# Own terms of a graph attention layer added behind the merge instead of inside it

## The chip, the cores and the metric

One core of one Trainium2 chip runs the whole program. The metric is the device time of one execution in microseconds (us), as the median of several executions. TensorE, VectorE, ScalarE, GpSimd and SyncE are called PE, DVE, ACT, POOL and SP, as in the profile.

## The reference, cut to what matters

Four graph layers follow each other on 3125 nodes with 256 features; 53125 edges (src, dst, sorted by dst) contain a self loop for each node. The change touches only the fourth, an attention layer with 8 heads of 32 features, which adds a self loop to each node once more:

```python
loop = jnp.arange(n); src = jnp.concatenate([src, loop]); dst = jnp.concatenate([dst, loop])
h = (x @ W).reshape(n, HEADS, OUT_DIM)
e = jax.nn.leaky_relu(a_src[src] + a_dst[dst], 0.2)
m = jax.ops.segment_max(e, dst, num_segments=n)
e = jnp.exp(e - m[dst])
denom = jax.ops.segment_sum(e, dst, num_segments=n)
alpha = e / (denom[dst] + 1e-16)
out = jax.ops.segment_sum(h[src] * alpha[:, :, None], dst, num_segments=n)
# + bias, an inner layernorm with gamma and beta, then layernorm(x + out)
```

The kernel takes this second self loop apart: for every node it adds an "own term", its own row h times exp(own score - maximum of its segment), to the sum over the listed edges. A row has 264 floats: 8 heads of 32 features and a 1 behind each, so that the denominator is summed beside the numerator.

## The kernel before

Nodes lie in 25 tiles of 128, edges in 416 tiles of 128; four edge tiles are a quad (104 quads). The last stage, the **merge**, sums weighted source rows into node tiles. For each quad the rows h[src] are brought into one of 16 row places (4 tiles, 528 KB). Places 1, 3, 5, ... 15 and 8 are staged: their rows were gathered early, kept in DRAM, and SP loads them back with one DMA each (`load_rows`, L2155). The seven other places are direct: POOL gathers their rows with four indirect DMAs for each quad (`gather_group`, L2105). A place is used again 16 quads later; `place_free` makes SP and POOL wait until `s_mm`, which PE counts up by one at every step (it starts at 8), shows that the old rows have been read: quad q waits for count 8 + 4(q - 16) + 3 + 25.

DVE weighs the rows of a quad in place (`scale_rows`, L2461) and builds onehot matrices for a group of four steps (`node_hots`, L2467), in two halves of one buffer, so group q waits until PE's count is 4q + 4, which is reached when group q - 2 is through. PE then does one fp32 matmul for each step (L2506, two instructions in the trace), 440 steps or 110 groups in all; a node tile is summed in one of four PSUM banks. ACT waits for the end of each node tile, copies its bank out (L2523) and prepares the bank of the node tile four further on. DVE's order is hots of group q, rows of quad q + 1, hots of group q + 1, and so on; nothing else stands in its queue until the last group.

The own term enters like this. Ahead of the merge each edge's segment maximum is written to DRAM. At the start of the merge POOL gathers first quads 6, 10, 12 and 14, then the maximum of each node tile (`gather_last`, L2428, 25 indirect DMAs), then makes the exponents (`weigh_own`, L2433 and L2435), and only then gathers the direct quads from 16 on. SP loads all own rows (3.3 MB, L2445) between the first and the second round of staged places. ACT takes the exponential (L2532) and weighs own rows by head (`weigh`, L2518, eight instructions for one node tile): those of tiles 8 to 24 straight into the bank, ahead of its sums, those of tiles 0 to 7 in place, beside copies of their sums, which DVE adds behind the merge (L2551).

Behind the merge `attended`, `inner_stats`, `inner_norm` and `store` run over groups of four node tiles, each stage one group behind the one before. DVE's order is attended(0); inner_stats(0), attended(1); inner_norm(0), inner_stats(1), attended(2); and so on. inner_norm(0) waits for a square root that ACT makes (L763), and ACT's root stands in its queue behind everything that `merge_act` issues.

## Time and profile before

| | |
|---|---|
| median of 3 executions | 3052.11 us (3040.15 to 3060.54) |
| the profiled execution, its own time | 3039.42 us |
| its span, first to last instruction | 3037.6 us |
| mean granted TensorE clock | 0.906 of full speed |
| merge, first weighing of rows to the last copy of a bank | 2625.5 to 2966.8 us |
| behind the merge | 2966.8 to 3037.6 us |
| busy share of the span | PE 81%, DVE 46%, POOL 31%, ACT 23% |

All places in time are microseconds from the start of the span. In a timeline a row gives start, duration, engine, line, operation, tiles, how many instructions are merged, and in brackets how long the engine was idle before it and who ended that. "remote" is an end of a wait for which the profile finds no instruction; "issue" is time without a wait that it shows. A DMA issued by POOL counts as busy only while its descriptors are made.

### The profile page before, as it was taken

Reading aid. Unit: us, or ns where it says so; the run is one execution under the profiler, and the core shown is the slowest. Engines: PE = TensorE matmul, PEld = TensorE weight load, DVE = VectorE, ACT = ScalarE, POOL = GpSimd, SP = SyncE. Lnnn points to the kernel's source line nnn. Section 1 sums busy time; section 2 is a strip of 40 time slices with the busy share of each in tenths; the row PEclk is TensorE's granted clock in tenths of the full one; section 3 lists DMA queues with packets and bytes.
Section 4 is the critical chain, followed back from the end, with each engine's and each line's share of the span. In section 5 each row is a group of like instructions: output and inputs, shape, how many; then the busy total and the mean of one; then the engine's idle time right before and its main releaser. Section 6 shows DMA issues by size and latency. Waiting matters only on the chain. (4 is left out here: it accounts for less than half of the span.)

```text
span 3037.6 us, 32378 instructions
## 1 busy us (share of the span) xinstructions
PE 2471.0 (81%) x9483; PEld 1629.1 (54%) x9484; DVE 1394.4 (46%) x3940; ACT 708.7 (23%) x1552; POOL 932.0 (31%) x927
## 2 busy tenths in 40 slices
PE   4777988996884999999999999999947787547680
PEld 2444977434763555565556555677723344435560
DVE  7998755455673001030101001455636555636568
ACT  3777644112442000010001000354400000103112
POOL 0000256665664300000000000012267665566640
PEclk8898998997996999999999999999978989769885
DMA  6656677343332544444444444333287888536541
GB/s 234 246 238 253 198 233 217 126 144 120 111 105 71 167 153 129 156 132 148 135 150 131 149 124 140 103 98 103 77 213 252 266 269 261 188 111 198 179 134 42
DMA packets 209534, 493.89 MB, mean 163 GB/s; under 512 B 46457, under 2 KB 128430, under 8 KB 209134
## 3 DMA queue, kind: packets, MB, share of 16 engines
q1 hardware_dynamic: 134353, 297.50, 30.6%
q10 hardware_dynamic: 39005, 137.07, 13.3%
q0 software_dynamic: 36032, 57.60, 7.1%
q8 instruction: 67, 1.10, 0.1%
q14 instruction: 77, 0.63, 0.1%
HBM read 374.71 MB, written 117.32 MB: 162 GB/s over the span
## 5 line engine op out<-in xcount | busy, mean ns | idle before, releaser
L792 POOL DMA_INDIRECT table_dense_weights<-pair_weight,dst x416 | 408.5, 982 | 607.8 <-DVE weights_c L845 350.6
L1522 PE MATMUL banks<-own_term,features_and_rows 128*128 128x391 f32 (+1 forms) x1656 | 552.3, 491 | 0.0
L2105 POOL DMA_INDIRECT features_and_rows<-table_heads,src x376 | 399.6, 1063 | 223.4 <-issue 105.8
L1522 PEld LDWEIGHTS banks<-own_term,features_and_rows 128*128 128x128 f32 x1656 | 312.2, 189 | 226.8
L1548 DVE TENSOR_SCALAR features_and_rows<-banks,hop_bias 128x391 f32<-128x391 f32 (+1 forms) x24 | 15.0, 624 | 780.2 <-PE banks L1522 780.2
L947 PE MATMUL banks<-split_rows,count_columns 128*128 128x512 f32 x1200 | 320.5, 415 | 17.5 <-issue 9.3
L2506 PE MATMUL banks<-features_and_rows,edge_to_window 128*128 x880 | 232.3, 426 | 107.9 <-DVE edge_to_window L2467 60.0
L1522 PE MATMUL banks<-features_and_rows 128*128 128x391 f32 (+1 forms) x840 | 282.4, 491 | 0.0
L947 PEld LDWEIGHTS banks<-split_rows,count_columns 128*128 128x128 f32 x1200 | 228.6, 194 | 70.9 <-issue 15.6
L2506 PEld LDWEIGHTS banks<-features_and_rows,edge_to_window 128*128 128x128 f32 x880 | 180.2, 209 | 159.9 <-issue 126.2
L558 PE MATMUL banks<-features_and_rows,pair_and_bias_rows 128*128 128x400 f16 x806 | 185.3, 395 | 85.4 <-DVE features_and_rows L540 41.3
L929 ACT CAST count_columns<-hidden 128x640 fp32r<-128x640 f16 x310 | 212.7, 723 | 144.5 <-PE banks L947 41.8
L1522 PEld LDWEIGHTS banks<-features_and_rows 128*128 128x128 f32 x840 | 158.4, 189 | 114.6
L2197 PE MATMUL banks<-features_and_rows,pair_weight 128*104 128x512 bf16 (+1 forms) x672 | 170.9, 395 | 58.8 <-issue 36.7
L1973 POOL DMA_INDIRECT ble_values_at_first_edge<-dst,row_of_first_edge x50 | 48.1, 961 | 515.1 <-DVE ln_rstd L1952 449.6
L1597 POOL DMA_INDIRECT features_and_rows<-table_hop,node_of_tail_row x6 | 5.7, 952 | 630.9 <-DMA table_hop<-tmp 609.6
L558 PEld LDWEIGHTS banks<-features_and_rows,pair_and_bias_rows 128*128 128x128 f16 x806 | 113.8, 152 | 157.2 <-issue 142.7
L540 DVE TENSOR_SCALAR features_and_rows<-counter_fp,features_and_rows 128x400 f16<-128x400 f16 x806 | 196.9, 320 | 0.0
L1539 ACT ACTIVATE features_and_rows<-banks,hop_bias 128x391 f32<-128x391 f32 (+1 forms) x24 | 14.1, 587 | 724.6 <-PE banks L1522 724.6
L2197 PEld LDWEIGHTS banks<-features_and_rows,pair_weight 128*104 128x104 bf16 x672 | 90.3, 138 | 161.0 <-issue 103.7
L1067 PE MATMUL banks<-split_rows,count_columns 128*128 128x258 f32 (+1 forms) x1200 | 160.7, 293 | 13.9 <-issue 9.3
L1067 PEld LDWEIGHTS banks<-split_rows,count_columns 128*128 128x128 f32 x1200 | 154.5, 199 | 18.0 <-issue 16.4
(425 smaller groups left out, 2985.8 us busy)
## 6 DMA issues: line engine op xcount, KB each, us to landing
hidden<-table_counts SPq DMA_DIRECT2D x305, 160.0 KB
table_dense_weights<-weights_c ACTq DMA_DIRECT2D x26, 1600.0 KB, 5.7
own_term<-table_dense_weights SPq DMA_DIRECT2D x52, 782.0 KB
features_and_rows<-table_rows_by_edge SPq DMA_DIRECT2D x58, 528.0 KB
pair_and_bias_rows<-table_edge_rows ACTq DMA_DIRECT2D x52, 512.0 KB
weights_c<-table_edge_rows ACTq DMA_DIRECT2D x52, 512.0 KB
own_term<-table_dense_weights SPq DMA_DIRECT2D x34, 780.5 KB
table_rows_by_edge<-features_and_rows SPq DMA_DIRECT2D x48, 528.0 KB
```

The lines of the kernel that those rows point to most:

```text
L540: made = e.tensor_scalar(hot_ring[:, s % HOTS, q, :], counter[:, 0:WIDE], steps_key[:, q, s:s + 1], None, ALU.is_equal)
L558: m = e.matmul(banks[:, bass.ds(bank_at, WIDE)], low_ring[:, s // LOWS_AT_ONCE % LOW_BLOCKS, :, 2 * (s % LOWS_AT_ONCE) + q], hot_ring[:, s ...
L792: e.indirect_dma_start(out=self.table, out_offset=bass.IndirectOffsetOnAxis(ap=self.place[:, t:t + 1], axis=0), in_=self.values[:, t:t + 1 ...
L929: e.copy(in_group(count_columns, g), in_group(slot_of(q), g)).then_inc(s_a_wide, 1)
L947: m = e.matmul(to[:, 0:2 * DIM], lhs_of(k), both_pieces(k), start=(k == first), stop=False, skip_group_check=True)
L1067: m = e.matmul(to(wide), count_columns[:, k, :], piece(k, h, wide), start=(k == 0 and h == 0), stop=False, skip_group_check=True)
L1522: m = e.matmul(psum[b][:, 0:wide], z_block(block)[:, f * P:(f + 1) * P], streamed[tile % STREAM][:, lo - from_column:lo - from_column + wi ...
L1548: e.tensor_scalar(xT[:, f, first:first + wide], psum[b][:, 0:wide], hop_bias[:, 0, hop * K_IN + f:hop * K_IN + f + 1], None, ALU.add).then ...
L1973: e.indirect_dma_start(out=t_start[c], out_offset=bass.IndirectOffsetOnAxis(ap=start_at[:, j:j + 1], axis=0), in_=node_pair[:, j, c * HEAD ...
L2105: e.indirect_dma_start(out=to[:, k, :], out_offset=None, in_=t_h, in_offset=bass.IndirectOffsetOnAxis(ap=src[:, t:t + 1], axis=0)).then_in ...
L2197: m = e.matmul(psum[i % 2][head_rows, 0:n], table[:, q, c, :], low_hot[i % 2][c][:, 0:n], start=(c == 0 and q == 0), stop=(c == 1 and q == ...
L2506: e.matmul(banks[:, bass.ds(column_at, ATT_ROW)], onehot[:, k % UNROLL, :], wide_rows[:, bass.ds(row_at, ATT_ROW)], start=False, stop=Fals ...
```

## The change

The segment maxima are gathered by POOL behind all direct quads, and the exponents are made in seven groups of four node tiles. The own rows are not loaded at the start; SP loads them group by group, behind the last staged quad, into places 8 to 14 as these become free (`load_own`, with the gate of quads 104 to 110). During the merge ACT only copies banks out and clears them. Behind node tile 22 it weighs the own rows of the first group, and behind the last node tile those of the six other groups, in place (`weigh(g)`); DVE adds them to the sums in each `attended(g)`.

```diff
@@ -52,7 +52,7 @@
 PLACES = 16
 ROW_BIT = 11
 SUM_BANKS = 4
-OWN_LATER = 8
+OWN_BEHIND = 22
 STEPS_A_LOAD = 20
 LOADS = 2
 STAGED_PLACES = tuple(sorted((*range(1, PLACES, 2), PLACES // 2)))
@@ -2022,7 +2022,6 @@
         last_projection, a_ok = (s_proj3, NODE_TILES), (s_head3, NODE_TILES)
         w_h = s_tab, pr.count.get(s_tab.name, 0) + 16 * NODE_TILES
         pr.count[s_tab.name] = w_h[1]
-        s_own_back = pr.sem("own_rows_back")
 
         begun_rows = (s_begun_rows, 2 * 16 * NODE_TILES)
 
@@ -2071,8 +2070,6 @@
         own_mem = own[:, :, :].rearrange("p t d -> p (t d)")
         bent_cut = lambda lo, n: own_mem[:, lo:lo + n]
         held_seen = pair_rows[:, 4 * DIM:4 * DIM + 2 * COLS].rearrange("p (b n) -> p b n", b=2)
-        first_sums = [at.rearrange("p (t c) -> p t c", c=ATT_ROW) for at in (
-            hidden[:, SCAN_LEN:SCAN_LEN + GROUP * ATT_ROW], w_a[:, 0:GROUP * ATT_ROW])]
         table = pair_weight[:, :].bitcast(BF16)[:, 0:TERMS * 2 * PICKED_ROWS].rearrange("p (q c n) -> p q c n", q=TERMS, c=2)
         by_dst, seg, prefix = agg[:, 0, :], agg[:, 1, :], agg[:, 2, :]
         max_all = prefix
@@ -2138,9 +2135,8 @@
                                              in_offset=bass.IndirectOffsetOnAxis(ap=row_first[:, c:c + 1], axis=0)).then_inc(s_first_value, 16)
             gather_direct(e, [q for q in DIRECT_QUADS if q < 2 * IN_CHAIN])
             gather_direct(e, [q for q in DIRECT_QUADS if 2 * IN_CHAIN <= q < PLACES])
+            gather_direct(e, [q for q in DIRECT_QUADS if q >= PLACES])
             gather_last(e)
-            weigh_own(e)
-            gather_direct(e, [q for q in DIRECT_QUADS if q >= PLACES])
 
         def keep_rows(e, some):
             for n in some:
@@ -2414,37 +2410,53 @@
 
         mx = tmp[:, 0, 0:NODE_TILES * HEADS].rearrange("p (t h) -> p t h", h=HEADS)
         own_gap = tmp[:, 1, 0:NODE_TILES * HEADS].rearrange("p (t h) -> p t h", h=HEADS)
-        s_last = pr.sem("segment_max_landed")
+        OWN_GROUPS = [range(lo, min(lo + GROUP, NODE_TILES)) for lo in range(0, NODE_TILES, GROUP)]
+        FIRST_OWN = 2
+        s_last = [pr.sem(f"segment_max_landed{b}") for b in range(2)]
+        s_own_back = [pr.sem(f"own_rows_back{b}") for b in range(2)]
+        in_part = lambda g: int(g >= FIRST_OWN)
         s_own_max = pr.sem("own_maximum_made")
         s_own_gap = pr.sem("own_exponent_made")
         s_self = pr.sem("own_weight_made")
         s_own_scaled = pr.sem("own_rows_scaled")
+        own_rows = lambda g: place[PLACES // 2 + g][:, 0:len(OWN_GROUPS[g]), :]
 
         def gather_last(e):
             e.wait_ge(*w_run)
             e.wait_ge(*zeroed_start)
             e.wait_ge(*rows_known)
-            for j in range(NODE_TILES):
-                e.indirect_dma_start(out=mx[:, j, :], out_offset=None, in_=t_run,
-                                     in_offset=bass.IndirectOffsetOnAxis(ap=last_at[:, j:j + 1], axis=0)).then_inc(s_last, 16)
-
-        def weigh_own(e):
-            e.wait_ge(*g_last)
-            e.tensor_tensor(mx, own_score, mx, ALU.subtract).then_inc(s_own_max, 1)
-            e.wait_ge(s_own_max, 1)
-            e.tensor_tensor(own_gap, mx, mask[:, :].unsqueeze(2).broadcast_to([P, NODE_TILES, HEADS]), ALU.mult).then_inc(s_own_gap, 1)
-
-        g_last = (s_last, 16 * NODE_TILES)
+            for g, tiles_of in enumerate(OWN_GROUPS):
+                for j in tiles_of:
+                    e.indirect_dma_start(out=mx[:, j, :], out_offset=None, in_=t_run,
+                                         in_offset=bass.IndirectOffsetOnAxis(ap=last_at[:, j:j + 1], axis=0)).then_inc(s_last[in_part(g)], 16)
+                if g == FIRST_OWN:
+                    for some in range(FIRST_OWN):
+                        weigh_own(e, some)
+            for g in range(FIRST_OWN, len(OWN_GROUPS)):
+                weigh_own(e, g)
+
+        def weigh_own(e, g):
+            lo, n = OWN_GROUPS[g][0], len(OWN_GROUPS[g])
+            e.wait_ge(s_last[in_part(g)], 16 * (NODE_TILES - FIRST_OWN * GROUP if in_part(g) else FIRST_OWN * GROUP))
+            e.tensor_tensor(mx[:, lo:lo + n, :], own_score[:, lo:lo + n, :], mx[:, lo:lo + n, :], ALU.subtract).then_inc(s_own_max, 1)
+            e.wait_ge(s_own_max, g + 1)
+            e.tensor_tensor(own_gap[:, lo:lo + n, :], mx[:, lo:lo + n, :],
+                            mask[:, lo:lo + n].unsqueeze(2).broadcast_to([P, n, HEADS]), ALU.mult).then_inc(s_own_gap, 1)
+
+        def load_own(e, g):
+            lo, n = OWN_GROUPS[g][0], len(OWN_GROUPS[g])
+            place_free(e, QUADS + g)
+            e.dma_start(own_rows(g), t_h[lo * P:(lo + n) * P, :].rearrange("(t p) d -> p t d", p=P)).then_inc(s_own_back[in_part(g)], 16)
 
 
         def attention_sp(e):
             keep_rows(e, range(STAGED))
             for quad in [q for q in STAGED_QUADS if q < PLACES]:
                 load_rows(e, quad)
-            e.wait_ge(*weights_made)
-            e.dma_start(own[:, :, :], t_h.rearrange("(t p) d -> p t d", p=P)).then_inc(s_own_back, 16)
             for quad in [q for q in STAGED_QUADS if q >= PLACES]:
                 load_rows(e, quad)
+            for g in range(len(OWN_GROUPS)):
+                load_own(e, g)
 
         s_begun = pr.sem("node_bank_begun")
         s_summed = pr.sem("node_tile_summed")
@@ -2512,28 +2524,28 @@
             ends_of_node = [e.alloc_register(f"node_end{k}") for k in range(NODE_TILES)]
             e.load(ends_of_node, merge_control[0:1, MERGE_STEPS:MERGE_STEPS + NODE_TILES])
 
-            def weigh(to, d, signal):
-                for h in range(HEADS):
-                    of = slice(h * HEAD_ROW, (h + 1) * HEAD_ROW)
-                    done = e.activation(to[:, of], own[:, d, of], ACT.Copy, scale=p_self[:, d, h:h + 1])
-                done.then_inc(signal, 1)
+            def weigh(g):
+                some = OWN_GROUPS[g]
+                e.wait_ge(s_own_gap, g + 1)
+                e.activation(p_self[:, some[0]:some[-1] + 1, :], own_gap[:, some[0]:some[-1] + 1, :], ACT.Exp).then_inc(s_self, 1)
+                e.wait_ge(s_self, g + 1)
+                e.wait_ge(s_own_back[in_part(g)], 16 * (len(OWN_GROUPS) - FIRST_OWN if in_part(g) else FIRST_OWN))
+                for d in some:
+                    for h in range(HEADS):
+                        of = own_rows(g)[:, d - some[0], h * HEAD_ROW:(h + 1) * HEAD_ROW]
+                        done = e.activation(of, of, ACT.Copy, scale=p_self[:, d, h:h + 1])
+                    done.then_inc(s_own_scaled, 1)
 
             for d in range(NODE_TILES):
                 e.wait_ge(s_mm, e.snap(ends_of_node[d], min_val=1, max_val=MERGE_STEPS + UNROLL))
-                e.copy(first_sums[d // GROUP][:, d % GROUP, :] if d < OWN_LATER else own[:, d, :], node_bank(d)).then_inc(s_summed, 1)
+                e.copy(own[:, d, :], node_bank(d)).then_inc(s_summed, 1)
                 if d + SUM_BANKS < NODE_TILES:
                     e.wait_ge(s_summed, d + 1)
-                    if d + SUM_BANKS < OWN_LATER:
-                        e.copy(node_bank(d + SUM_BANKS), no_sums).then_inc(s_begun, 1)
-                    else:
-                        if d + SUM_BANKS == OWN_LATER:
-                            e.wait_ge(s_own_gap, 1)
-                            e.wait_ge(s_own_back, 16)
-                            e.activation(p_self, own_gap, ACT.Exp).then_inc(s_self, 1)
-                            e.wait_ge(s_self, 1)
-                        weigh(node_bank(d + SUM_BANKS), d + SUM_BANKS, s_begun)
-                        if d + SUM_BANKS < 2 * OWN_LATER:
-                            weigh(own[:, d + SUM_BANKS - OWN_LATER, :], d + SUM_BANKS - OWN_LATER, s_own_scaled)
+                    e.copy(node_bank(d + SUM_BANKS), no_sums).then_inc(s_begun, 1)
+                if d == OWN_BEHIND:
+                    weigh(0)
+            for g in range(1, len(OWN_GROUPS)):
+                weigh(g)
 
         pr.queue["sp"].append(attention_sp)
         pr.queue["pe"].append(merge_pe)
@@ -2546,11 +2558,9 @@
         def attended(g):
 
             den = tiles(a_dst, g)
-            t = None
-            if g[-1] < OWN_LATER:
-                t = V(lambda e: e.tensor_tensor(tiles(own, g), tiles(own, g), first_sums[g[0] // GROUP][:, :, :], ALU.add),
-                      (s_own_scaled, g[-1] + 1), (s_summed, g[-1] + 1))
-            t = V(lambda e: e.tensor_scalar(den, tiles(h_rows, g)[:, :, :, HEAD_DIM], 1e-16, None, ALU.add), (s_summed, g[-1] + 1), t)
+            t = V(lambda e: e.tensor_tensor(tiles(own, g), tiles(own, g), own_rows(g[0] // GROUP), ALU.add),
+                  (s_own_scaled, g[-1] + 1), (s_summed, g[-1] + 1))
+            t = V(lambda e: e.tensor_scalar(den, tiles(h_rows, g)[:, :, :, HEAD_DIM], 1e-16, None, ALU.add), t)
             t = V(lambda e: e.reciprocal(den, den), t)
             for j in g:
                 t = V(lambda e, j=j: e.tensor_tensor(heads(spare[:, j, :]), h_rows[:, j, :, 0:HEAD_DIM],
```

## Rows read from the trace of the kernel before

**Rows 1.** By stretch: us, then busy PE, PEld, DVE, ACT, POOL; clock, DMA share, GB/s.
```profile
2625.50:2966.80 341.30, 232.94 (x884) 180.54 (x884) 195.71 (x220) 57.45 (x236) 209.48 (x199) 0.84 0.55 171
...
2656.00:2706.00 50.00, 12.54 (x27) 7.70 (x25) 6.11 (x7) 0.76 (x2) 34.75 (x37) 0.50 0.23 56
...
2966.80:3037.60 70.80, 0.00 (x0) 0.00 (x0) 61.30 (x207) 18.73 (x41) 0.00 (x0) 0.51 0.14 46
```

**Rows 2.** Waits in the merge, longest in total: us, times, longest.
```profile
DVE edge_to_window L2467 <- remote: 94.1, 13, 15.7
```

**Rows 3.** DVE's timeline in the merge: hots of groups 10 to 13.
```profile
2658.52 0.69 DVE L2467 TENSOR_TENSOR edge_to_window<-banks,dst_of_step 128x512 f32<-128x512 f32 x1 [3.82 <-issue]
...
2676.02 0.69 DVE L2467 TENSOR_TENSOR edge_to_window<-banks,dst_of_step 128x512 f32<-128x512 f32 x1 [15.65 <-remote]
...
2692.15 0.69 DVE L2467 TENSOR_TENSOR edge_to_window<-banks,dst_of_step 128x512 f32<-128x512 f32 x1 [14.27 <-remote]
...
2705.45 0.69 DVE L2467 TENSOR_TENSOR edge_to_window<-banks,dst_of_step 128x512 f32<-128x512 f32 x1 [11.45 <-remote]
```

**Rows 4.** PE's timeline in the merge: steps of group 9, group 11, groups 13 to 19.
```profile
2653.87 3.04 PE L2506 MATMUL banks<-features_and_rows,edge_to_window 128*128 x8 [2.25 <-issue]
...
2677.06 3.88 PE L2506 MATMUL banks<-features_and_rows,edge_to_window 128*128 x8 [13.62 <-issue]
...
2706.49 14.13 PE L2506 MATMUL banks<-features_and_rows,edge_to_window 128*128 x56 [9.42 <-DVE edge_to_window L2467]
```

**Rows 5.** SP's timeline: load of the own rows, load of staged quad 19.
```profile
2633.98 0.45 SPq L2445 DMA_DIRECT2D own_term<-table_heads  x1
...
2676.01 0.32 SPq L2155 DMA_DIRECT2D features_and_rows<-table_rows_by_edge  x1
```

**Rows 6.** POOL's timeline: maxima first and last, quads 16 to 20, last quad.
```profile
2653.15 0.94 POOL L2428 DMA_INDIRECT tmp<-table_running_max,row_of_last_edge  x1 [0.30 <-issue]
...
2683.99 0.94 POOL L2428 DMA_INDIRECT tmp<-table_running_max,row_of_last_edge  x1 [0.30 <-issue]
...
2687.66 0.98 POOL L2105 DMA_INDIRECT features_and_rows<-table_heads,src  x1
...
2701.45 0.95 POOL L2105 DMA_INDIRECT features_and_rows<-table_heads,src  x1 [0.30 <-issue]
...
2935.08 0.95 POOL L2105 DMA_INDIRECT features_and_rows<-table_heads,src  x1 [0.30 <-issue]
```

**Rows 7.** DVE's timeline near the end of the merge: hots of groups 96 and 97.
```profile
2930.03 0.69 DVE L2467 TENSOR_TENSOR edge_to_window<-banks,dst_of_step 128x512 f32<-128x512 f32 x1 [6.08 <-remote]
...
2938.45 0.69 DVE L2467 TENSOR_TENSOR edge_to_window<-banks,dst_of_step 128x512 f32<-128x512 f32 x1 [6.56 <-remote]
```

**Rows 8.** PE's timeline, end of the merge: groups 97 to 104, 105 to 109.
```profile
2939.48 17.56 PE L2506 MATMUL banks<-features_and_rows,edge_to_window 128*128 x64 [4.62 <-DVE edge_to_window L2467]
...
2957.61 9.16 PE L2506 MATMUL banks<-features_and_rows,edge_to_window 128*128 x40 [0.57 <-issue]
```

**Rows 9.** ACT's timeline: exponential and weighing of two node tiles; behind the merge.
```profile
2726.40 0.37 ACT L2532 ACTIVATE weights_c<-tmp 128x200 f32<-128x200 f32 x1
...
2726.80 1.78 ACT L2518 ACTIVATE banks<-own_term,weights_c 128x33 f32<-128x33 f32 x8
...
2728.52 1.80 ACT L2518 ACTIVATE own_term<-own_term,weights_c 128x33 f32<-128x33 f32 x8
...
2966.80 0.38 ACT L2523 COPY own_term<-banks 128x264 f32<-128x264 f32 x1 [3.18 <-PE banks L2506]
...
2967.20 1.28 ACT L763 ACT_TABLE_LOAD   x1
...
2969.59 0.30 ACT L763 ACTIVATE ln_rstd<-ln_mean_var,eps 128x4 f32<-128x4 f32 x1 [1.10 <-DVE ln_mean_var L762]
```

**Rows 10.** DVE's timeline behind the merge: attended(0), start of inner_norm(0).
```profile
2963.86 1.25 DVE L2551 TENSOR_TENSOR own_term<-own_term,hidden 128x1056 f32<-128x1056 f32 x1
...
2972.77 0.17 DVE L2565 RECIPROCAL ln_rstd<-ln_rstd 128x4 f32<-128x4 f32 x1
```

## The prediction

> **What bounds the kernel now.** I read the page first, then the busy time by stretch, the waits, and last the timelines of each engine through the merge. The merge takes 341.3 us of the 3037.6 us span, and no engine is busy in all of it: PE 232.9 us, POOL 209.5 us, DVE 195.7 us, ACT 57.5 us [rows 1]. So it is bounded by waits. The largest is DVE's before its hots, 94.1 us in 13 waits, ended by something that the profile cannot name [rows 2]. Three of them, 15.65, 14.27 and 11.45 us, follow each other before groups 11, 12 and 13, in a stretch of 50 us in which PE is busy for 12.5 us [rows 1, 3].
>
> What are they waits for? The hots of group 11 need PE's count at 48, which is 40 steps, groups 0 to 9. Group 9's eight instructions began at 2653.87 and took 3.04 us, so they had run by 2656.9; but the hots started at 2676.02 [rows 3, 4]. SP's load of quad 19 has the same gate, 8 + 12 + 28 = 48, and was issued at 2676.01 [rows 5]. Two engines that wait for the same count go on in the same 10 ns, 19 us after the steps are through. So the wait is for PE's count, and the count arrives late. It isn't bytes: DMA moves 56 GB/s in that stretch, against 171 GB/s over the merge [rows 1].
>
> What makes it late? All through those waits POOL issues indirect DMAs without a pause: the 25 of the maxima, whose first and last begin at 2653.15 and 2683.99 (30.84 / 24 = 1.28 us from one to the next), and quads 16, 18 and 20 follow from 2687.66 to 2702.40; the last of the three waits ends 3.0 us later, at 2705.45 [rows 3, 6]. The same happens without the maxima, only shorter: near the end POOL's last gather ends at 2936.03, and DVE, which had waited 6.08 and 6.56 us for groups 96 and 97, goes on at 2938.45, 2.4 us later [rows 6, 7]. After it the PE runs undisturbed. I read this as: while POOL issues indirect DMAs in one long streak, PE's counts trickle in, one group in about 16 us (2676.02 to 2692.15), and they arrive at once when it pauses. Direct quads are gated by that same count, so such a streak ends itself. The gather of the maxima has no such gate.
>
> Here the Trainium skill speaks otherwise. "SBUF — State Buffer", section on who interferes with whom, says in a sentence that PE and ACT never wait on anyone, and "TensorE: Matmul & The Clock Gate", on the semaphore tail, puts the cost of one increment at about 26 ns. The 16 us for four counts in the row contradict both as a description of this merge. With them the moved gathers would cost nothing in either place; what that gives is the first rival.
>
> Behind the merge the bound is DVE, 61.3 us busy of 70.8 [rows 1].
>
> **Part 1, the front of the merge: 34 us less.** Out of POOL's queue ahead of quad 16 go 25 indirect DMAs, their landing, and two small operations. Quad 16's gather can then start where the maxima did, at 2653.15 instead of 2687.66: 34.5 us earlier [rows 6]. Quads 16 and 18 are 8 gathers, 10 us. Quad 20 must wait for count 8 + 16 + 28 = 52, so POOL pauses near 2663, and the counts arrive some 2.4 to 3 us later, as in rows 3, 6 and 7: hots of group 11 near 2666 instead of 2676.02. Groups 12 and 13 then follow at 2.0 us (14.13 us for seven groups, [rows 4]) to 3.7 us, so that group 13 comes near 2672, against 2705.45: 33 us. The 3.3 MB of own rows leave the same stretch too (issued at 2633.98, [rows 5]), worth about 1 us more of earlier landings. I take 34. Bounds: 10 if only the first of the three waits shrinks (2676.0 to 2666), and 46 if all 41.4 us of them go and loads come 5 us sooner. From then on POOL is the slower partner as before, so I leave the other ten waits alone.
>
> **Part 2, the end of the merge: 27 us more.** The 25 gathers now follow the last quad without a gate, from 2936.03 (place in the old time), for 25 x 1.28 = 32 us, with two pairs of small operations after the twelfth, about 2 us, to about 2970. DVE's hots of group 97 would have waited until 2938.45; now the counts go on trickling, one group in 13 to 16 us [rows 3], so that only groups 97 and 98 come through by 2970. Flush at 2972, and 11 groups remain. The 13 groups from 97 on took 2939.48 to 2966.77, 27.3 us [rows 8]; 11 take 23.1 us. 2973 + 23 = 2996, 29 us behind 2966.8; the short pause after the twelfth gather gives back perhaps 2. Bounds: nothing, if the maxima's gathers don't hold counts back, and 34 us, the whole streak. I take 27, near the upper end, because the longest of all waits in the trace stand beside just these 25 gathers.
>
> The exponents (a group's two operations on POOL, then ACT's) are ready by about 2975, before ACT needs them. SP's seven loads have gates from count 388 to 412, the last after step 404, group 100, which now runs near 2977; four loads of 528 KB at 171 GB/s [rows 1] take 12 us, to 2989. ACT needs group 2's rows at 3001 and later. All hidden; if they weren't, up to 5 us. The clear of a bank by a copy is cheaper than the weighing into it, and PE did not wait for that, so 0.
>
> **Part 3, behind the merge: 40 us more.** ACT weighed 136 of its instructions into banks and 64 in place, all beside PE. One node tile takes 2728.52 - 2726.80 = 1.72 us [rows 9]. Behind the last copy there are now 21 node tiles, 36.1 us, and six exponentials, 0.40 us each to the next start [rows 9], 2.4 us: 38.5 us. The group weighed behind node tile 22 lies beside PE's last 20 us and costs 0. Only then come ACT's table load, 1.28 us, and the first root. In the trace the last copy starts at 2966.80 and inner_norm(0) at 2972.77, 6.0 us later [rows 9, 10]. After the change it is 0.4 + 38.5 + 1.3 + 0.3 = 40.5 us. DVE can do attended(0), inner_stats(0) and attended(1) in that time, and then it waits, since all else stands behind inner_norm(0). That is 34.6 us. The rest of DVE's work follows unshortened, with 4 additions more of 1.25 us (as attended(0)'s, [rows 10]) and one of a quarter: 5.3 us, since groups 0 and 1 had theirs before. Sum 39.9. Bounds 35 (additions partly beside waits) and 45 (waits between groups of ACT instructions).
>
> **Sum.** -34 + 27 + 40 = +33 us. Profiled execution: 3039.4 + 33 = 3072. That execution lies 12.7 us below the median shown, 3052.1, against which the change is measured: 3085. The runs of before spread over 20 us, so I take 1%, 30.5 us, as what can be told from no change.
>
> **Rivals.**
> - *The gathers at the end hold nothing back.* The late counts at the front come from what is special there (six staged loads, own rows and gathers at once up to 2656), and the end of the merge keeps its pace: -34 + 0 + 40 = +6, 3058. This is the not slower side. It decides if the counts flow while POOL gathers maxima. For it: near the end hots of groups 96 and 97 waited 6 us, not 15 [rows 7]. Against it: DMA is almost idle in the long waits. The two sentences of the skill would lead here.
> - *The front stall stays.* If streaks of 8 and 16 gathers are enough, group 11's wait shrinks and the others come back at quads 20 and 22: -10 + 27 + 40 = +57, 3109. Against it: direct quads are gated.
> - *Faster:* POOL runs ahead for good, is always stopped by its gate, and long streaks vanish from the whole merge. 94.1 - 41.4 = 52.7 us more would go: -34 - 53 + 27 + 40 = -20, 3032, and 3005 with a free end as well. It decides if POOL keeps ahead of PE; but a direct quad takes 4 x 1.28 = 5.1 us at least, 7 of 16 are direct, so 2.2 us for each group against PE's 2.0 [rows 4]: POOL falls behind wherever PE runs well.
> - *The change doesn't do what it says:* own rows land after ACT asks for them. They have 12 us of slack above; 5 us at most.
>
> **How the numbers follow.** Forecast 0.55, own range 3070 to 3100, a little over half of it beyond 1%. Free end 0.25, 3058. Front stall stays 0.13, 3109. Faster 0.07, half of it at 3005, the rest at 3032, within 1%. Range for 8 in 10: 3048 to 3108, which takes in the free end and leaves out half of the two outer cases. Slower by over 1%: 0.30 + 0.13 and a little, 0.44. Faster by over 1%: 0.04. Within 1%: 0.52.
>
> **What would show it.** Right: POOL's gather of maxima as the last of its queue, with DVE's hots of groups 96 to 98 waiting 13 us each beside it; the waits of groups 11 to 13 down to under 10 us in all; behind the last copy a block of 168 ACT instructions of 38 us, in which DVE is idle for about 32 us before inner_norm(0). Wrong: hots at every 2 us beside the maxima's gathers; or long waits at the front as before. What would make the prediction wrong is above all part 2, which rests on a reading of two coincidences.

## The result, and the profile after

The changed kernel takes 3084.78 us (median of 4, 3083.64 to 3087.02); the kernel before, beside it, 3046.13 us (median of 4, 3035.96 to 3060.54). The ratio is 1.0113, with a 95% interval of 1.0081 to 1.0146, so it is slower, and whether by more than 1% is open. The forecast was 3085. The profiled execution took 3083.64 us, with a span of 3081.8 us against 3037.6 us before: 44.2 us more.

Busy time by stretch of the kernel after: us, then busy PE, PEld, DVE, ACT, POOL; clock, DMA share, GB/s. The lines answer to [rows 1].

```profile
2636.50:2972.00 335.50, 235.13 (x884) 182.34 (x884) 196.15 (x221) 26.26 (x85) 216.51 (x211) 0.84 0.55 174
...
2898.00:2950.00 52.00, 13.14 (x34) 8.82 (x35) 7.68 (x9) 0.67 (x2) 37.09 (x49) 0.60 0.28 75
2971.90:3081.80 109.90, 0.00 (x0) 0.00 (x0) 67.02 (x212) 55.85 (x215) 0.00 (x0) 0.52 0.09 29
```

The 52 us near the end look like the 50 us near the start in [rows 1]: PE busy for 13.1 us, POOL for 37.1 us, DMA at 75 GB/s. The hole has moved from one end of the merge to the other. Behind the merge DVE is busy for 67.0 of 109.9 us, against 61.3 of 70.8.

DVE's timeline in the kernel after, hots of groups 11 to 13, answering to [rows 3], then of groups 96 to 100, answering to [rows 7].

```profile
2674.66 0.69 DVE L2479 TENSOR_TENSOR edge_to_window<-banks,dst_of_step 128x512 f32<-128x512 f32 x1
...
2677.67 0.69 DVE L2479 TENSOR_TENSOR edge_to_window<-banks,dst_of_step 128x512 f32<-128x512 f32 x1 [1.15 <-PE banks L2518]
...
2679.45 0.69 DVE L2479 TENSOR_TENSOR edge_to_window<-banks,dst_of_step 128x512 f32<-128x512 f32 x1
...
2903.22 0.69 DVE L2479 TENSOR_TENSOR edge_to_window<-banks,dst_of_step 128x512 f32<-128x512 f32 x1 [4.87 <-remote]
2914.55 0.69 DVE L2479 TENSOR_TENSOR edge_to_window<-banks,dst_of_step 128x512 f32<-128x512 f32 x1 [9.47 <-remote]
2933.49 0.69 DVE L2479 TENSOR_TENSOR edge_to_window<-banks,dst_of_step 128x512 f32<-128x512 f32 x1 [17.08 <-remote]
2948.23 0.69 DVE L2479 TENSOR_TENSOR edge_to_window<-banks,dst_of_step 128x512 f32<-128x512 f32 x1 [12.89 <-remote]
2950.01 0.68 DVE L2479 TENSOR_TENSOR edge_to_window<-banks,dst_of_step 128x512 f32<-128x512 f32 x1
```

POOL's timeline after: the first gather behind a gate, one gather of maxima in each of the two streaks at the end, and the last operation on exponents. PE's timeline after: steps of groups 96 to 98, then the rest.

```profile
2668.78 0.95 POOL L2102 DMA_INDIRECT features_and_rows<-table_heads,src  x1 [6.11 <-PE banks L2518]
...
2910.79 0.95 POOL L2430 DMA_INDIRECT tmp<-table_running_max,row_of_last_edge  x1 [0.30 <-issue]
...
2942.33 0.94 POOL L2430 DMA_INDIRECT tmp<-table_running_max,row_of_last_edge  x1 [0.30 <-issue]
...
2947.01 0.20 POOL L2443 TENSOR_TENSOR tmp<-tmp,has_edges 128x8 f32<-128x8 f32 x1
```

```profile
2904.26 2.72 PE L2518 MATMUL banks<-features_and_rows,edge_to_window 128*128 x8 [4.09 <-DVE edge_to_window L2479]
2915.59 3.77 PE L2518 MATMUL banks<-features_and_rows,edge_to_window 128*128 x8 [8.61 <-DVE edge_to_window L2479]
2934.53 3.88 PE L2518 MATMUL banks<-features_and_rows,edge_to_window 128*128 x8 [15.16 <-DVE edge_to_window L2479]
2949.27 12.90 PE L2518 MATMUL banks<-features_and_rows,edge_to_window 128*128 x48 [10.86 <-DVE edge_to_window L2479]
```

The reading is that of the front before. The hots of group 98 need the count of group 96, whose matmuls had run by 2904.26 + 2.72 = 2906.98; they started at 2933.49, 26.5 us later. Those of group 99 need group 97, run by 2915.59 + 3.77 = 2919.36, and started at 2948.23, 28.9 us later. (The profile models the ends of matmuls, so "had run" is only as good as that.) All that time POOL issued indirect DMAs, the maxima's from 2910.79 on, the last one from 2942.33 to 2943.27. 5 us later the counts are there, and DVE goes on every 1.8 us. A pause of 1.3 us in POOL's gathers, from 2925.98 to 2927.30, did not bring them.

ACT's timeline after, from the last copy of a bank on, answering to [rows 9]; then DVE's first addition and the start of inner_norm(0), answering to [rows 10].

```profile
2971.92 0.38 ACT L2541 COPY own_term<-banks 128x264 f32<-128x264 f32 x1 [3.18 <-PE banks L2518]
...
2972.46 6.92 ACT L2536 ACTIVATE features_and_rows<-features_and_rows,weights_c 128x33 f32<-128x33 f32 x32
...
3007.80 1.82 ACT L2536 ACTIVATE features_and_rows<-features_and_rows,weights_c 128x33 f32<-128x33 f32 x8
3009.63 1.28 ACT L763 ACT_TABLE_LOAD   x1
```

```profile
2979.41 1.26 DVE L2561 TENSOR_TENSOR own_term<-own_term,features_and_rows 128x1056 f32<-128x1056 f32 x1 [4.81 <-ACT features_and_rows L2536]
...
3011.26 0.18 DVE L2575 RECIPROCAL ln_rstd<-ln_rstd 128x4 f32<-128x4 f32 x1 [28.51 <-ACT ln_rstd L763]
```

ACT is in one piece of work from 2971.92 to the table load at 3009.63, 37.7 us. DVE waits for it twice, 4.8 and 28.5 us.

Where the 44.2 us of span went, in the two profiled executions:

| stretch | before, us | after, us | difference | forecast |
|---|---|---|---|---|
| start to the hots of group 0 | 2626.7 | 2637.5 | +10.7 | 0 |
| hots of group 0 to those of group 13 | 78.7 | 42.0 | -36.7 | -34 |
| hots of group 13 to those of group 95 | 216.2 | 216.7 | +0.5 | 0 |
| hots of group 95 to those of group 109 | 41.6 | 72.2 | +30.6 | +27 |
| hots of group 109 to the last copy of a bank | 3.6 | 3.6 | 0 | 0 |
| last copy to the end of the span | 70.8 | 109.9 | +39.1 | +40 |

The first row is taken as no effect of the change, whose code begins with the merge. In the traces of the experiments below, which don't touch the code ahead of the merge either, the hots of group 0 start anywhere from 2613.9 to 2653.2 us (f2 aside), and the kernel before ranges over 24.6 us here. Without that row the sum is 33.5 us, against 33 forecast.

### The profile page after: what moved, and what is told of

Same layout as the page of the kernel before. It is cut to its first block and busy times, and to the rows that moved or that the text cites. A ratio compares the mean times of both kernels' runs of the same rounds, so it can differ in the third digit from the quotient of the medians.

```text
span 3081.8 us, 32433 instructions
## 1 busy us (share of the span) xinstructions
PE 2465.7 (80%) x9483; PEld 1618.0 (53%) x9484; DVE 1402.1 (45%) x3945; ACT 713.6 (23%) x1575; POOL 947.6 (31%) x939
## 3 DMA queue, kind: packets, MB, share of 16 engines
q10 hardware_dynamic: 39005, 137.07, 12.9%
## 5 line engine op out<-in xcount | busy, mean ns | idle before, releaser
L2102 POOL DMA_INDIRECT features_and_rows<-table_heads,src x376 | 406.6, 1081 | 211.8 <-issue 109.8
```

The lines of the kernel that those rows point to most:

```text
L2102: e.indirect_dma_start(out=to[:, k, :], out_offset=None, in_=t_h, in_offset=bass.IndirectOffsetOnAxis(ap=src[:, t:t + 1], axis=0)).then_in ...
```

## The experiments

All times are medians, each beside runs of the kernel before on the same chip at the same time. Those lay at 3046 to 3051 us for after, the a's and b1, at 3032 for the c's, d1 and the e's, and at 2812 for f2, while the expectations name times on the level of 3046 to 3051: only the ratios and differences can be compared. Where a length of the merge is given below, it runs from the hots of group 0 to the start of the last matmul.

| kernel | this, us | before, us | ratio, 95% interval |
|---|---|---|---|
| after | 3084.78 | 3046.13 | 1.0113, 1.0081 to 1.0146 |
| a1: maxima first | 3097.29 | 3051.25 | 1.0151, 1.0114 to 1.0188 |
| a2: DVE weighs | 3067.43 | 3051.25 | 1.0047, 1.0017 to 1.0077 |
| a3: one count a group | 3089.86 | 3051.25 | 1.0124, 1.0087 to 1.0161 |
| b1: the same in the kernel before | 3056.25 | 3051.25 | 1.0014, 0.9994 to 1.0035 |
| c1: maxima paced | 3050.01 | 3032.23 | 1.0069, 1.0041 to 1.0097 |
| c2: arithmetic for the maxima | 3048.45 | 3032.23 | 1.0048, 1.0015 to 1.0080 |
| c3: plain DMAs for the maxima | 3028.87 | 3032.52 | 0.9996, 0.9964 to 1.0027 |
| c4: a2, maxima spread | 3052.95 | 3032.23 | 1.0063, 1.0031 to 1.0096 |
| d1: a2, five places for hots | 3009.32 | 3032.23 | 0.9933, 0.9899 to 0.9967 |
| e1: d1 and c1 | 2999.90 | 3032.52 | 0.9902, 0.9867 to 0.9937 |
| e2: e1 and a3 | 3004.23 | 3032.52 | 0.9894, 0.9839 to 0.9948 |
| f2: d1, more matmuls | 2803.68 | 2811.76 | 0.9972, 0.9955 to 0.9990 |

### a1: the maxima gathered first again, all else as after

```diff
-            gather_direct(e, [q for q in DIRECT_QUADS if q >= PLACES])
             gather_last(e)
+            gather_direct(e, [q for q in DIRECT_QUADS if q >= PLACES])
```

> The changed kernel with the maxima's 25 gathers put back ahead of quad 16, own rows still loaded and added behind the merge. Theory (a long ungated streak of indirect DMAs holds PE's counts back, wherever it stands): groups 11 to 13 wait 40 us again, the end of the merge runs at 2 us for each group, the merge takes 335 to 345 us as before, the block behind it stays; total within 10 us of the changed kernel's 3085. Rival (the 3.3 MB of own rows at the front were what held the counts): the front stays free without them and the end becomes free too, 30 to 36 us less, 3050.

DVE's timeline in a1, hots of groups 8 to 11.

```profile
2682.26 0.69 DVE L2479 TENSOR_TENSOR edge_to_window<-banks,dst_of_step 128x512 f32<-128x512 f32 x1 [6.64 <-remote]
2695.64 0.69 DVE L2479 TENSOR_TENSOR edge_to_window<-banks,dst_of_step 128x512 f32<-128x512 f32 x1 [11.53 <-remote]
2714.66 0.69 DVE L2479 TENSOR_TENSOR edge_to_window<-banks,dst_of_step 128x512 f32<-128x512 f32 x1 [17.16 <-remote]
2716.43 0.68 DVE L2479 TENSOR_TENSOR edge_to_window<-banks,dst_of_step 128x512 f32<-128x512 f32 x1
```

The stall is back at the front without the load of the own rows, 35.3 us in three waits, before groups 8 to 10, and the end is free: groups 95 to 109 take 27.8 us. So it goes with the gathers, wherever they stand. The total came 12 us above the changed kernel's, where within 10 was said; with 1.0151 against 1.0113 and overlapping intervals the two aren't told apart.

### a2: DVE weighs the own rows

ACT only makes the exponentials. In `attended(g)` DVE multiplies the group's rows by the weights, broadcast over the 33 columns, ahead of its addition.

```diff
-                for d in some:
-                    for h in range(HEADS):
...
-                        done = e.activation(of, of, ACT.Copy, scale=p_self[:, d, h:h + 1])
...
+            t = V(lambda e: e.tensor_tensor(rows3, rows3, p, ALU.mult), (s_self, k + 1), ...)
             t = V(lambda e: e.tensor_tensor(tiles(own, g), tiles(own, g), own_rows(k), ALU.add), t, (s_summed, g[-1] + 1))
```

> The changed kernel with the own rows weighed by DVE, one multiplication for each group of four node tiles in attended, in place of 32 ACT instructions; ACT keeps the exponentials. Theory (ACT's block of 38 us ahead of the first root sets the stage behind the merge): that stage falls from 110 us to 84 (70.8 before, 5.3 of additions, 6.3 x 1.25 of multiplications), 3059. Rival (DVE would wait for something else there, the own rows' landing or the exponents): less than 10 us gained.

The stretch behind the last copy of a bank falls from 109.9 to 84.5 us, as the theory had it. One multiplication of 128x1056 takes DVE 1.24 us; the same product took ACT 32 instructions and 6.92 us.

### a3 and b1: PE counts once for a group

```diff
-                    e.matmul(...).then_inc(s_mm, 1)
+                    m = e.matmul(...)
+                    if k % GROUP == GROUP - 1:
+                        m.then_inc(s_mm, GROUP)
```

> The changed kernel with PE counting once for each group of four steps, by 4, in place of once for each step. Theory (counts are delivered one by one, slowly, while POOL issues indirect DMAs): with a quarter of them the long waits shrink to a quarter or less; 84 us of waits without a named end, so 50 to 75 us less, 3010 to 3035. Rival 1 (all counts are held until POOL pauses, however many): no change, 3085. Rival 2 (PE itself is slow, in its clock or its reads): no change either, with PE's steps slow.

> The same edit in the kernel before: 94 us of waits without a named end, 60 to 80 us less by the theory, 2970 to 2990. By the rivals no change, 3046.

DVE's timeline in a3, hots of groups 97 to 99, and PE's, steps of groups 95 to 97.

```profile
2923.04 0.69 DVE L2479 TENSOR_TENSOR edge_to_window<-banks,dst_of_step 128x512 f32<-128x512 f32 x1 [10.97 <-remote]
2940.62 0.69 DVE L2479 TENSOR_TENSOR edge_to_window<-banks,dst_of_step 128x512 f32<-128x512 f32 x1 [15.73 <-issue]
2956.75 0.69 DVE L2479 TENSOR_TENSOR edge_to_window<-banks,dst_of_step 128x512 f32<-128x512 f32 x1 [14.27 <-remote]
```

```profile
2906.47 2.04 PE L2518 MATMUL banks<-features_and_rows,edge_to_window 128*128 x8 [0.72 <-issue]
2911.26 3.45 PE L2518 MATMUL banks<-features_and_rows,edge_to_window 128*128 x8 [2.75 <-issue]
2924.08 3.86 PE L2518 MATMUL banks<-features_and_rows,edge_to_window 128*128 x8 [9.38 <-DVE edge_to_window L2479]
```

One count for a group is as late as four: 14.5, 25.9 and 28.8 us behind the matmuls that it reports. Neither time changed beyond its interval: 1.0124 against 1.0113, and 1.0014 for b1. My idea that each count is slow to deliver fell.

### c1: each four maxima behind a gate; c4: one behind each direct quad

```diff
             for g, tiles_of in enumerate(OWN_GROUPS):
+                e.wait_ge(s_mm, mm0 + (94 + 2 * g) * GROUP)
```

> The changed kernel with a gate on PE's count ahead of every four of the maxima's gathers, from group 94 on, every two groups. Theory (an ungated streak is what makes the waits long; a gate makes POOL pause, and then the counts come through): no wait beyond 10 us at the end, 12 to 22 us less, 3063 to 3073. Rival (it is the number of gathers beside the last groups that counts): within 5 us of 3085.

```diff
+            for n, quad in enumerate([q for q in DIRECT_QUADS if q >= PLACES]):
+                gather_direct(e, [quad])
+                if n < NODE_TILES:
+                    gather_last(e, n)
```

> a2_dve_weigh with the 25 gathers of maxima spread, one behind each direct quad from 16 on. Theory: the end of the merge keeps 2 us for each group, 25 to 30 us less there, of which the longer pace of POOL in the middle (5 instead of 4 DMAs for each direct quad, 32 us over the merge) takes back 10 to 30; 3045 to 3065 against 3067. Rival (the cost goes with the number of indirect DMAs issued without a pause anywhere, so it is only moved): 3067.

In c1 the longest step from one group to the next at the end is 7.1 us, against 18.9, and the merge takes 311.0 us against 334.0. The times say less: 1.0069 against 1.0113, with intervals that overlap. In c4 the end is free (39.1 us from group 95 to 109), but three waits of 11.5 to 12.9 us stand in the middle of the merge: 339.5 us, against 338.3 in a2. Between two gates POOL now issued five gathers instead of four. The cost was moved, not removed, as the rival had it: 1.0063, against 1.0047 for a2.

c1 also shows that a streak does not make the stall at once. There POOL issued 48 indirect DMAs without a pause from 2664.8 to 2736.1, and groups 8 to 34 came on at 2.3 us each until 2724.1. In the changed kernel the streak that ends in the hole began at 2870.4, and groups 82 to 95 still followed at 2.0 us until 2896.1. What sets the moment at which PE falls behind, no run here shows.

### c2 and c3: something else in the place of the 25 gathers

```diff
-                    e.indirect_dma_start(out=mx[:, j, :], ...)
+                    for k in range(2):
+                        e.tensor_tensor(rest_of_tmp, own_score, own_score, ALU.add)...
+                    e.tensor_copy(mx[:, j, :], own_score[:, j, :])...
```

> The changed kernel without the gather of the maxima: in place of each of the 25 indirect DMAs POOL runs two additions of 200 columns and a small copy, about as long in all. It leaves the maxima out (own scores stand for them). Theory (indirect DMAs issued in a row hold back PE's counts): with the same time of plain arithmetic the groups from 97 on come every 2 us, the end of the merge is 25 to 30 us shorter, 3055. Rival (a busy POOL of any kind, or something else at the end of the merge): groups 97 to 99 wait 10 to 19 us each as before, 3085.

```diff
-                    e.indirect_dma_start(out=mx[:, j, :], ...)
+                    e.dma_start(rest_of_tmp[:, j, :], t_run[j * P:(j + 1) * P, :])...
+                    e.tensor_copy(mx[:, j, :], own_score[:, j, :])...
```

> The changed kernel with 25 plain DMAs issued by POOL in place of the 25 indirect ones, of 128 rows of 32 bytes too; it leaves the maxima out (own scores stand for them). Theory (descriptors made by POOL, for whatever DMA, hold back PE's counts): groups 97 to 99 wait 10 to 19 us each if the plain DMAs take POOL as long, and less in proportion if they take less. Rival (only indirect DMAs do): end of the merge as in c2_compute, 30 us shorter than in the changed kernel.

Both kernels leave the maxima out, so their times are no times of a usable kernel. Only the end of the merge is read.

POOL's timeline in c2 and DVE's beside it, hots of groups 97 to 99.

```profile
2902.82 0.94 POOL L2102 DMA_INDIRECT features_and_rows<-table_heads,src  x1 [0.30 <-issue]
2903.77 1.13 POOL L2434 TENSOR_TENSOR tmp<-dst 128x200 f32<-128x200 f32 x2
```

```profile
2904.27 0.69 DVE L2484 TENSOR_TENSOR edge_to_window<-banks,dst_of_step 128x512 f32<-128x512 f32 x1 [7.31 <-issue]
2906.54 0.69 DVE L2484 TENSOR_TENSOR edge_to_window<-banks,dst_of_step 128x512 f32<-128x512 f32 x1 [0.41 <-PE banks L2523]
2909.07 0.69 DVE L2484 TENSOR_TENSOR edge_to_window<-banks,dst_of_step 128x512 f32<-128x512 f32 x1 [0.68 <-PE banks L2523]
```

POOL's timeline in c3.

```profile
2896.48 0.96 POOL L2102 DMA_INDIRECT features_and_rows<-table_heads,src  x1 [0.30 <-issue]
2897.44 0.61 POOL L2433 DMA_DIRECT2D tmp<-table_running_max  x1
```

In c2 the last indirect DMA ends at 2903.76 and DVE goes on 0.5 us later; in c3 it ends at 2897.44, and DVE goes on at 2897.60. From there the groups keep their pace, while POOL stays busy. Groups 95 to 109 take 39.7 and 39.5 us, against 72.2. So neither a busy POOL nor its plain DMAs do it; indirect DMAs do. c2's work takes POOL as long as the gathers, 1.4 us for each maximum. c3's plain DMAs are shorter, 0.6 us each, and all 25 with their copies take about 20 us against 32; plain DMAs for as long as the gathers were not run.

### d1: three more places for hots

DVE may be five groups of hots ahead instead of two; the three new places lie in the tile weights_a, which is free in the merge. The kernel is a2 otherwise.

```diff
-            if not (isinstance(quad, int) and quad < 2):
-                e.wait_ge(s_mm, quad * GROUP + (mm0 - GROUP))
+            if quad >= len(hot_slot):
+                e.wait_ge(s_mm, mm0 + (quad - len(hot_slot) + 1) * GROUP)
```

> a2_dve_weigh with five places for the onehots of a group instead of two, so that DVE waits for the count of group q - 5, not q - 2 (DVE's loop is written out). Theory A (counts are late by 12 to 29 us but PE itself runs on): PE gets three groups further in each stretch of late counts, 6 us in each of six or seven, 25 to 40 us less, 3030 to 3042. Theory B (PE's own steps are slow in those stretches): no more than a few us, 3060 to 3067.

The merge falls from 338.3 to 311.5 us, the gain that theory A had named. But its premise, that PE itself runs on, does not hold beside the last maxima. PE's timeline in d1 beside the last maxima, its weight loads there (PEld), and DVE's next hots.

```profile
2907.30 0.60 PE L2513 MATMUL banks<-features_and_rows,edge_to_window 128*128 x1 [1.28 <-issue]
2910.10 0.60 PE L2513 MATMUL banks<-features_and_rows,edge_to_window 128*128 x1 [2.20 <-issue]
2912.90 0.60 PE L2513 MATMUL banks<-features_and_rows,edge_to_window 128*128 x1 [2.20 <-issue]
```

```profile
2908.70 0.29 PEld L2513 LDWEIGHTS banks<-features_and_rows,edge_to_window 128*128 128x128 f32 x1 [1.82 <-issue]
2911.51 0.29 PEld L2513 LDWEIGHTS banks<-features_and_rows,edge_to_window 128*128 128x128 f32 x1 [2.52 <-issue]
```

```profile
2922.72 0.69 DVE L2481 TENSOR_TENSOR edge_to_window<-banks,dst_of_step 128x512 f32<-128x512 f32 x1 [20.56 <-issue]
```

The same line's register operations on PE's sequencer (the part of PE that issues its instructions) in d1: ns, minimum, median and maximum, and where. First from 2906.5 to 2922.6, then from 2870 to 2882.

```profile
L2513 PEldq FUSED_REGOPS  x4: 690/700/700, 2906.6 to 2915.0; - x4
...
L2513 PEldq FUSED_REGOPS  x19: 138/138/420, 2870.2 to 2880.9; - x19
```

With hots ready, PE still issues a matmul, a weight load, a matmul, each 1.40 us behind the last, and idles between them for no wait. A register operation takes 0.70 us instead of 0.14. The clock is too small a reason: it is granted at 0.50 there (1.2 GHz) and at 1.00 from 2870 to 2882, but a matmul comes in 2.80 us against 0.26 (46 in 12.0 us), ten times as long. So in d1 it isn't the count alone that is late: PE's whole stream of instructions is slow. A group has 16 of them (8 matmuls, 8 weight loads), and 16 x 1.40 = 22.4 us is the step between two hots in d1 (2900.31 to 2922.72). After's 18.94 us (2914.55 to 2933.49) would be 1.18 us for each, and before's 16.13 [rows 3] 1.01. That is a guess from d1: after's own trace has a group's eight matmuls within 3.8 us, and no register operation of that line above 0.164 us in the whole merge. With two groups of hots, either PE's work or only its count is late there, and the traces don't tell which.

The gain of d1 comes ahead of the maxima. Up to group 95 PE is 25.4 us sooner than in a2, counted from its first step, and from there to the last matmul it gains 1.5 us more.

### e1 and e2: five places and the gates of c1, then also one count a group

The edits are those of c1 and a3, made in d1.

> d1_five_hots with the gates of c1_paced ahead of every four maxima. In d1_five_hots groups 100 to 102 still wait 15, 22 and 5 us beside the maxima. Theory (an ungated streak makes the long waits, five places bridge the short ones; the two are separate): the end loses another 15 to 25 us, ratio to before 0.985 to 0.989. Rival (five places already bridge what the gates save): within 5 us of d1_five_hots, 0.992 to 0.995.

> e1_five_hots_paced with one count for each group of four steps. Theory (a count's lateness doesn't depend on how many there are, as a3_count_by_group showed): within 5 us of e1_five_hots_paced. Rival (with more groups under way the number of counts matters after all): 10 us or more less.

e1 takes 286.2 us for the merge and 0.9902 of before; it beats the kernel before, and with it the changed one. The ratio lies between what the theory (0.985 to 0.989) and the rival (0.992 to 0.995) had said. Its interval overlaps d1's, so that the gates add something on top is seen in the traces (311.5 to 286.2) but not settled by the times. e2 is the same as e1 within the noise (4.3 us apart).

### f2: a small matmul more in each step of d1

```diff
+                    e.matmul(banks[:, bass.ds(column_at, 1)], zeros_b[:, :], zeros_b[:, 0:1], start=False, stop=False, skip_group_check=True)
```

> The kernel with five places for the hots (d1), with one small matmul more per step: weights of zeros, one column, added ahead of the step's own matmul into the same bank, so that it adds nothing. In d1's trace, beside the last maxima, PE has hots ready and still issues a weight load, a matmul, a weight load and so on 1.40 us apart (2908.70, 2910.10, 2911.51, 2912.90), one group's 16 in 22.4 us, which I had not looked at before. Theory: what is slow beside a streak of indirect DMAs is each instruction of PE, whichever it is; then the added weight load and matmul also take about 1.4 us each, a step with 6 instructions takes 8.4 us instead of 5.6, and a group 28 to 34 us instead of 22. Rival: a fixed delay for each step (its reads of registers, its waits, its count) that is only spread over its instructions; then a step stays at 5.6 us and the distances between the instructions shrink to about 0.9 us. In both, PE's ordinary pace also falls, by 0.1 to 0.2 us a step, 440 steps: 30 to 90 us of the merge are possible, if PE becomes its bound; ratio to before 1.00 to 1.03.

The question was not answered, since the stall was not there to be measured. Beside f2 the kernel before took 2811.76 us, on the chip on which it took 3032.52 us beside the e's; all other comparisons here lie at 3032 to 3051. POOL's timeline in f2 with the first and the last gather of maxima, and PE's beside them.

```profile
2689.80 0.95 POOL L2430 DMA_INDIRECT tmp<-table_running_max,row_of_last_edge  x1 [0.30 <-issue]
...
2723.22 0.94 POOL L2430 DMA_INDIRECT tmp<-table_running_max,row_of_last_edge  x1 [0.30 <-issue]
```

```profile
2698.62 0.17 PE L2513 MATMUL banks<-zeros_bf 128*128 128x1 bf16 x1
2699.18 0.17 PE L2513 MATMUL banks<-zeros_bf 128*128 128x1 bf16 x1
```

Beside 25 gathers at about the pace of the changed kernel ((2723.22 - 2689.80) / 24 = 1.39 us, against 1.31), PE takes 0.56 us for a step (2698.62 to 2699.18), more instructions and all. DVE has no wait ended by "remote" in the merge, though POOL issued 196 indirect DMAs without a pause, from 2428.0 to 2705.4.

f2's own edit is not the reason for the new level: the kernel before, without it, was 220.8 us faster too, and most of f2's gain lies in code ahead of the merge, which d1 has word for word. POOL's indirect DMAs of an early stage, matmuls of a long stage with only six of them, and matmuls of the stage ahead of the merge, in d1, then in f2: ns, and first and last start.

```profile
L792 POOL DMA_INDIRECT table_dense_weights<-pair_weight,dst x416: 965/971/2530, 348.3 to 1023.6; - x139
L1522 PE MATMUL banks<-own_term,features_and_rows x1656: 487/491/575, 1041.9 to 1955.8; 128*128 128x391 f32 x161, 128*128 128x388 f32 x23
L2193 PE MATMUL banks<-features_and_rows,pair_weight x672: 270/379/669, 2229.5 to 2600.7; 128*104 128x512 bf16 x144, 128*104 128x256 bf16 x24
```

```profile
L792 POOL DMA_INDIRECT table_dense_weights<-pair_weight,dst x416: 963/968/2529, 350.3 to 919.0; - x139
L1522 PE MATMUL banks<-own_term,features_and_rows x1656: 487/491/575, 909.3 to 1823.2; 128*128 128x391 f32 x161, 128*128 128x388 f32 x23
L2193 PE MATMUL banks<-features_and_rows,pair_weight x672: 270/379/668, 2098.3 to 2404.9; 128*104 128x512 bf16 x144, 128*104 128x256 bf16 x24
```

The stage with 416 indirect DMAs of POOL's takes 675.3 us in d1 and 568.7 in f2. The long stage takes 913.9 us in both. The stage ahead of the merge, where POOL begins the gathers of L2102, takes 371.2 and 306.6 us. So the two levels differ where POOL issues many indirect DMAs, and not where it issues few. What these DMAs cost depends on a condition of the chip that the kernel doesn't set. That f2's merge has no stall fits this; a run of d1 or of the changed kernel on that level, which would settle it, was not made.

## Why the prediction was right

**Part 1, -34, measured -36.7.** Right in size, by a path that was only half the one forecast. POOL does pause at a gate, idle for 6.11 us up to 2668.78, and groups 10 to 13 follow at 1.8 to 3.0 us. But it is the gate of quad 16 (count 36, group 6), which the maxima had hidden before. Quad 20, at which the prediction had POOL stop, started 0.3 us after the DMA ahead of it, and from 2668.8 to 2719.8 POOL issued 36 indirect DMAs in one streak. Groups 11 to 13 got through because they stood at its start. That the number fits so well is in part luck. Two shorter waits, 3.86 and 6.78 us, stand ahead of the pause, before groups 5 and 6, where the kernel before had none. The other waits ended by "remote" I had left alone: between groups 13 and 95 they were 40.1 us before and are 29.5 us after (4.56, 8.78, 6.01, 10.12). That did not shorten the stretch (+0.5), so they are partly exchanged for waits with a named end. a1 shows the cause by putting the gathers back.

**Part 2, +27, measured +30.6.** Right in size, and the wait is the one forecast. DVE waited 4.87, 9.47, 17.08 and 12.89 us before groups 96 to 99, where 13 us each were said for 96 to 98; the 44.3 us in all stand against 12.6 at this end before [rows 7]. (The working flushes at 2972 and goes on from 2973, a slip of 1 us.) c1, c2 and c3 show that the 25 indirect gathers are the cause: with them paced or replaced, the merge is 23 to 35 us shorter. The mechanism, "PE's counts trickle in" for as long as a streak lasts, named the symptom. The runs with one count a group changed nothing, d1 shows PE itself issuing one instruction in 1.40 us, and c1 shows 59 us of a streak beside which the counts came on time. The prediction weighed a sentence of the Trainium skill ("SBUF — State Buffer", who interferes with whom: PE and ACT never wait on anyone). It speaks of the ports of SBUF, and no run here shows a port as the cause. Taken for PE as a whole, as the prediction took it, d1's trace is against it, where PE issues late beside POOL's gathers; f2's trace agrees with it, at 0.56 us a step.

**Part 3, +40, measured +39.1.** ACT's block was 37.7 us for 38.5 forecast, DVE's idle time 33.3 for 32. a2 confirms it from the other side: without ACT's 168 instructions, and with DVE's multiplications in their place, 25.4 us go. The loads of own rows were hidden, as said: SP issued the first at 2903.22, and ACT waited for none of them.

**The level.** The sum was placed on the median of three runs, 3052.1; four runs gave 3046.1. So 38.7 us of measured change met a forecast of 33, and the two errors cancelled in the figure of 3085.

**The rivals.** The free end would have needed PE to run through the last gathers. It did not in the executions compared, but in the condition of f2 it does. There parts 1 and 2 should both vanish and part 3 stay; after was not run in it, so that is argued, not shown. The rival in which POOL runs ahead for good did not come either, though one streak at the front was 36 DMAs long.

**Open.** Why indirect DMAs from POOL slow PE's stream, when in a streak it begins, and what differs on a chip where they don't. It is not the number of counts (a3, b1, e2), not POOL's arithmetic (c2), not its plain DMAs (c3, 0.6 us each), and hardly bytes (75 GB/s in the hole, against 174 over the merge). Whether the price is for each instruction or each step of PE was to come from f2 and stays open.

## What to carry to other kernels

Work moved out of a bad place takes its stall with it, if the stall comes from the work: ask what the moved instructions do to other engines, and whether anything gates them. Where the stall can't be removed, a deeper buffer in front of the engine that stalls (five places for hots) gave back 27 us of the merge, nearly all of it ahead of the longest stall, and gates that break up the streak 23; spreading the gathers gave nothing. Work on small pieces that ACT hides beside a long stage is cheap only there: behind the stage, 168 instructions of 0.216 us stood alone on the path, and one DVE instruction with a broadcast operand replaced 32 of them.

## What the hardware showed that I had not expected

Late in an unbroken streak of POOL's indirect DMAs, one in 1.25 us, PE issued an instruction in 1.40 us in d1 with nothing to wait for, and its register operations took 0.70 instead of 0.14 us. 25 plain DMAs from POOL, 0.6 us of POOL each, did nothing of the kind in c3. The same kernel took 3032.5 us and, later, 2811.8 on the same chip. Between d1 and f2 the difference lies in the stages in which POOL issues indirect DMAs (675.3 against 568.7 us for one with 416 of them), and a stage of 913.9 us with only six is the same in both. A comparison holds only beside runs of the same time and chip, and a mechanism found in one such condition may be absent in another.
